# Six accumulation banks for the open chunks of the first propagation of batch 0, and a new place for its transposed means

## The reference

```
h  = relu(layernorm(x))
Xw = h @ Wv + bv;  sj = Xw @ aw[:d];  si = Xw @ aw[d:]
T  = adj * exp(leaky_relu(sj[j] + si[i] + ab));  T = T / (rowsum(T) + 1e-12)
H  = h @ Wk0 + bk0 + (T h) @ Wk1 + bk1 + (T T h) @ Wk2 + bk2
x1 = x + relu(H)
h  = relu(layernorm(x1));  A = adj + I;  dh = rsqrt(rowsum(A))
out = x1 + relu((dh A dh) h @ kernel + bias)
```

## Time and profile before

| | us |
|---|---|
| median of 3 runs (763.99 to 766.89) | 764.09 |
| the profiled execution | 765.5 |
| its span | 763.7 |
| TensorE busy | 749.1 (98%) |
| VectorE busy | 623.8 (82%) |
| ScalarE busy | 536.9 (70%) |
| GpSimd busy | 187.1 (24%) |

### The profile page before, as it was taken

How to read it: one execution, slowest core, us unless ns; L and a number is a source line. 1 busy time by engine, 2 the same in 40 slices (tenths; PEclk the granted TensorE clock), 3 DMA queues, 4 the chain that set the end, 5 groups by cost and what they waited for, 6 DMA issues and landing times.

```text
span 763.7 us, 14034 instructions
## 1 busy us (share of the span) xinstructions
PE 749.1 (98%) x5099; PEld 689.8 (90%) x5099; DVE 623.8 (82%) x1417; ACT 536.9 (70%) x1044; POOL 187.1 (24%) x190
## 2 busy tenths in 40 slices
PE   8879999999999999999999999999999999999997
PEld 8778998999889898998979999899998999889986
DVE  7877888978888789887998879897888877986665
ACT  3887796667966689557885678856696677956451
POOL 3023141222403224041321304122140222402330
PEclk9989999999999999999999999999999999999999
DMA  6557348753486445872657625776248654455511
GB/s 223 211 183 251 115 163 277 224 203 129 156 284 210 174 153 172 284 248 85 194 186 266 231 77 189 241 258 223 95 155 275 214 208 139 156 184 183 168 64 55
DMA packets 63909, 143.32 MB, mean 188 GB/s; under 512 B 6768, under 2 KB 32864, under 8 KB 63840
## 3 DMA queue, kind: packets, MB, share of 16 engines
q1 hardware_dynamic: 55072, 111.75, 43.9%
q10 hardware_dynamic: 8768, 30.68, 11.4%
HBM read 133.96 MB, written 8.45 MB: 186 GB/s over the span
## 4 chain that ended last, share of the span: by engine, by line
PE 94%; DVE 3%; ACT 1%; issue 1%; DMA 0%; POOL 0%; POOLq 0%; DVEq 0%; ACTq 0%
PE acc L1176 15%; PE acc L1178 15%; PE acc L1177 15%; PE da L1044 14%; PE db L1044 8%; PE da L1142 4%; PE tp L1142 4%; PE da L1144 4%; PE da L1143 4%; PE tp L1144 4%; PE tp L1143 4%; PE acc L1076 1%; PE acc L1195 1%; DVE t_raw L806 1%; PE acc L1197 1%
## 5 line engine op out<-in xcount | busy, mean ns | idle before, releaser
L1176 PE MATMUL acc<-g_hi,t_hi 128*128 128x256 f32 (+1 forms) x976 | 276.6, 283 | 0.1
L1178 PE MATMUL acc<-g_hi,t_lo 128*128 128x256 f32 (+1 forms) x976 | 275.2, 282 | 0.0
L1177 PE MATMUL acc<-g_lo,t_hi 128*128 128x256 f32 x976 | 274.6, 281 | 0.0
L1177 PEld LDWEIGHTS acc<-g_lo,t_hi 128*128 128x128 f32 x976 | 184.3, 189 | 0.4
L1176 PEld LDWEIGHTS acc<-g_hi,t_hi 128*128 128x128 f32 x976 | 183.8, 188 | 0.9 <-DVE g_lo L780 0.3
L1178 PEld LDWEIGHTS acc<-g_hi,t_lo 128*128 128x128 f32 x976 | 184.1, 189 | 0.0
L398 POOL TENSOR_TENSOR g_lo<-tmp,g_hi 128x256 fp32r<-128x256 f32 x64 | 61.9, 967 | 266.4 <-ACT g_hi L578 266.4
L817 DVE TENSOR_TENSOR a_lo<-a_raw,a_hi 128x512 fp32r<-128x512 f32 x128 | 94.1, 750 | 23.9 <-ACT a_hi L566 23.8
L523 ACT ACTIVATE tg_e<-si,sij 128x256 f32<-128x256 f32 x256 | 109.5, 501 | 0.1
L566 ACT CAST a_hi<-a_raw 128x512 fp32r<-128x512 f32 x128 | 76.8, 618 | 26.0 <-DVE a_raw L856 17.9
L404 POOL TENSOR_TENSOR hs_lo<-tmp,hs_hi 128x256 fp32r<-128x256 f32 x64 | 60.0, 957 | 89.7 <-ACT hs_hi L463 89.7
(11 more groups left out here) (153 smaller groups left out, 1615.4 us busy)
## 6 DMA issues: line engine op xcount, KB each, us to landing
a_raw<-adj_dram SPq DMA_DIRECT2D x64, 512.0 KB, 4.4
a_raw<-adj_z_dram SPq DMA_DIRECT2D x64, 512.0 KB, 4.3
tg_a<-adj_t_dram ACTq DMA_DIRECT2D x58, 512.0 KB, 4.3
x_o<-x_dram SPq DMA_DIRECT2D x64, 128.0 KB, 3.5
out_dram<-x_o SPq DMA_DIRECT2D x64, 128.0 KB, 4.0
x_nat<-x_dram SPq DMA_DIRECT2D x28, 256.0 KB, 4.9
xt<-x_t_dram SPq DMA_DIRECT2D x28, 256.0 KB, 5.4
si<-mean_rows_dram SPq DMA_DIRECT2D x7, 512.0 KB, 4.6
```

Source lines behind the costliest of these rows:

```text
L1176: nc.tensor.matmul(acc[:, s, 0:n], l_hi, r_hi, start=(jt == 0), stop=False)
L1177: nc.tensor.matmul(acc[:, s, 0:D], l_hi, r_lo, start=False, stop=False)
L1178: ins = nc.tensor.matmul(acc[:, s, 0:n], l_lo, r_hi, start=False, stop=(jt == NT - 1))
```

## The change

Chunks of phase U in batch 0 go round six banks, the three of `acc` and then `db`, `da` 0 and `da` 1, by a function `first_acc`; VectorE reads them there. In `accumulate_halves`, which only batch 0 uses, a chunk now waits for the read of the chunk six before it. The dense products of batch 1, which write `da` and `db`, begin only after six chunks of batch 0 have been read. The transpose of the means is issued between the second halves of chunks 2 and 3, not ahead of chunk 2's; ScalarE's copy of them is after `leaky(0, 6)`, not ahead of it. Other batches keep their banks.

```diff
+        FB = AB + OB
+
+        def first_acc(i):
+
+            return [acc[:, s] for s in range(AB)][i % FB] if i % FB < AB else out_bank[i % FB - AB]
...
             for u in range(HJ, NU - 1):
+                leaky(0, u)
                 if u == NU - 2:
                     mean_copy(1)
-                leaky(0, u)
                 exponent(0, u)
                 t_high(0, u - 1, False)
...
             def u_chunk(b, i):
-                s, a = i % 2, acc_slot(U_PHASE, i)
+                s = i % 2
+                ps = first_acc(i) if b == 0 else acc[:, acc_slot(U_PHASE, i)]
...
                 if b > 1:
 
                     pe.wait_ge(z_tmp_done, (b - 1) * NT)
+                else:
+
+                    pe.wait_ge(g1_tmp_ready, FB)
                 for g in range(NG):
...
-            def accumulate_halves(b, cp, middle):
+            def accumulate_halves(cp, middle):
 
                 for jh in range(2):
-                    pe.wait_ge(t_ready, b * NU + 2 * cp + jh + 1)
-                    if jh == 1 and middle is not None:
-                        middle()
+                    pe.wait_ge(t_ready, 2 * cp + jh + 1)
                     for i in (2 * cp, 2 * cp + 1):
-                        s = acc_slot(U_PHASE, i)
-                        if jh == 0 and i >= AB:
-                            pe.wait_ge(g1_tmp_ready, b * NT + i - AB + 1)
-                        elif jh == 0 and b > 0:
-                            pe.wait_ge(v_tmp_done, b * NT + i - AB + 1)
+                        if jh == 1 and i % 2 and middle is not None:
+                            middle()
+                        s = first_acc(i)
+                        if jh == 0 and i >= FB:
+                            pe.wait_ge(g1_tmp_ready, i - FB + 1)
```

More of the change, by code:

```diff
@@ L820, in u_chunk @@
             def u_chunk(b, i):
-                s, a = i % 2, acc_slot(U_PHASE, i)
+                s = i % 2
+                ps = first_acc(i) if b == 0 else acc[:, acc_slot(U_PHASE, i)]
                 dve.wait_ge(acc_full, b * PHASES + i + 1)
-                nc.vector.tensor_scalar_add(row_t[:, i:i + 1], acc[:, a, D:D + 1], EPS_ROW).then_inc(row_t_done, 1)
+                nc.vector.tensor_scalar_add(row_t[:, i:i + 1], ps[:, D:D + 1], EPS_ROW).then_inc(row_t_done, 1)
                 dve.wait_ge(row_t_done, b * NT + i + 1)
@@ L830, in u_chunk @@
                     dve.wait_ge(g1_ready, b * NT + i - 1)
-                nc.vector.scalar_tensor_tensor(out=tmp[:, s, :], in0=acc[:, a, 0:D], scalar=rinv[:, i:i + 1],
+                nc.vector.scalar_tensor_tensor(out=tmp[:, s, :], in0=ps[:, 0:D], scalar=rinv[:, i:i + 1],
                                                in1=p1[:, i, :], op0=ALU.mult, op1=ALU.add).then_inc(g1_tmp_ready, 1)
@@ L1179, in accumulate @@
                 ins.then_inc(acc_full, 1)
-            def accumulate_halves(b, cp, middle):
+            def accumulate_halves(cp, middle):
                 for jh in range(2):
-                    pe.wait_ge(t_ready, b * NU + 2 * cp + jh + 1)
-                    if jh == 1 and middle is not None:
-                        middle()
+                    pe.wait_ge(t_ready, 2 * cp + jh + 1)
                     for i in (2 * cp, 2 * cp + 1):
-                        s = acc_slot(U_PHASE, i)
-                        if jh == 0 and i >= AB:
-                            pe.wait_ge(g1_tmp_ready, b * NT + i - AB + 1)
-                        elif jh == 0 and b > 0:
-                            pe.wait_ge(v_tmp_done, b * NT + i - AB + 1)
+                        if jh == 1 and i % 2 and middle is not None:
[3 more added lines that the diff above has]
+                            pe.wait_ge(g1_tmp_ready, i - FB + 1)
                         for jt in range(jh * HJ, (jh + 1) * HJ):
                             l_hi, l_lo = t_hi[:, i, jt, :], t_lo[:, i, jt, :]
-                            nc.tensor.matmul(acc[:, s, 0:D + 2], l_hi, g2_hi[:, jt, :], start=(jt == 0), stop=False)
-                            nc.tensor.matmul(acc[:, s, 0:D], l_hi, g2_lo[:, jt, :], start=False, stop=False)
-                            ins = nc.tensor.matmul(acc[:, s, 0:D + 2], l_lo, g2_hi[:, jt, :], start=False, stop=(jt == NT - 1))
+                            nc.tensor.matmul(s[:, 0:D + 2], l_hi, g2_hi[:, jt, :], start=(jt == 0), stop=False)
+                            nc.tensor.matmul(s[:, 0:D], l_hi, g2_lo[:, jt, :], start=False, stop=False)
+                            ins = nc.tensor.matmul(s[:, 0:D + 2], l_lo, g2_hi[:, jt, :], start=False, stop=(jt == NT - 1))
                         if jh == 1:
@@ L1208, in batch @@
                         if i % 2 == 0:
-                            accumulate_halves(b, i // 2, (lambda: rows_of_mean(b + 1)) if b == 0 and i == 2 else None)
+                            accumulate_halves(i // 2, (lambda: rows_of_mean(1)) if i == 2 else None)
                         continue
```

## The result

The median went from 764.04 us (762.69 to 766.89, 6 runs) to 759.71 us (759.06 to 759.82, 6 runs): ratio 0.9942, 95% interval 0.9925 to 0.9959, so 4.3 us or 0.58% faster. The profiled execution took 759.82 us with a span of 758.0 (before: 765.5 and 763.7), 5.7 us less.

A forecast was written before the change was run, and what follows sets the result against it. TensorE alone bounds everything behind 67.7 us. 7.79 us of old waits and echoes go, less 1.2 of new waits and 0.54 at the dense stage; 6.1 us taken, forecast 758.0 us, range 756.6 to 760.9.

The forecast's parts named there:

- (c): Rival, chance 0.05: units of t stay late because their loads time them; only the second wait and echo go, 761 us.
- (d): Rival, chance 0.03, slower: the clock stays at 1.2 GHz from 48.1 on, dense stage 1.3 us later than before, 765.4 us.
- The two bank waits and their echoes go: TensorE, batch 0's first propagation: waits of 2.73 and 2.23 us for tmp and slow-clock echoes of 1.26 and 1.57 vanish, 7.79 us.
- Pair (2, 3), and the pause at 48: TensorE runs chunks 2 and 3 without waiting for the means, then idles 0.9 us at 48.1 for unit 4's low part.
- That a pause of 1 us leaves the clock: TensorE's new idle of 0.9 us at 48.1 is too short to drop the granted clock from 1.00.
- rival (a): Rival, chance 0.20: one of TensorE's new pauses drops the clock for some 3 us, time 758.8 to 759.6 us.
- ScalarE's queue: ScalarE loses its 3.53 us idle: unit 6's leaky pieces start at 44.94, mean copy follows, unit 6's high part from 51.77.
- VectorE's steps of 1.14 us and GpSimd's of 1.66: VectorE's products and low parts take 1.14 us, GpSimd's splits 1.66; TensorE's next waits for t are 0.1 and 0.2 us.
- The start of the dense stage: Batch 1's dense stage starts at 61.45 in place of 67.66, 6.2 us earlier, after a wait of 1.25 us for ht_lo.
- The new wait for six reads: Ahead of batch 1's dense stage: met at 58.2, while TensorE arrives at 60.2, so it costs nothing.
- Row tile 4 late, rival (b): Rival, chance 0.10: row tile 4's load lands late, ScalarE's second ht_hi up to 1.5 us late, time 759.5 us.
- From profile to median: Profiled time forecast at 759.4 us; the median before lay 1.4 us under its profiled execution, which gives 758.0.

The follow-up runs named there:

- E2: The two moves of the means alone (transpose and ScalarE's copy), on the kernel before with its three banks: 763.97 us, ratio 0.9994 to the kernel before.
- E1: The change with its six banks alone, the transpose and ScalarE's copy of the means put back in their old places: 759.62 us.
- E3: The whole change with four banks (acc and db) in place of six, the wait for all eight reads ahead of the first product into db: 759.55 us.
- E4: The whole change, with GpSimd's splits of chunks 0 and 1 placed in VectorE's reads of chunks 1 and 2: 758.91 us.
- E5: The whole change, with batch 1's first ht pair ahead of less urgent work on ScalarE and VectorE, row sums 3 and 4 one chunk later: 760.99 us.
- E7: E6 with batch 1's transposed x loaded behind unit 7's adjacency tile in place of after unit 4's: 761.71 us.
- E9: The whole change, with ScalarE's first ht_hi of batch 1 just ahead of row sum 3 and VectorE's first ht_lo ahead of its second centring: 760.26 us.
- E8: The whole change, with TensorE also waiting for chunk 1's read ahead of pair (4, 5), a pause of 1.83 us: 759.68 us.
- E11: The whole change, with TensorE waiting ahead of pair (4, 5) for VectorE's product of unit 6, a pause of 2.94 us in the profile: 761.47 us.
- E6: The whole change with the edits of E4 and E5 together: 759.52 us.
- E10: E4 and E9 together, plus, in batch 1, VectorE's third centring behind its first read of db and ScalarE's third ht_hi behind its second tile: 758.51 us.

## Why the prediction was right

Forecast 758.0 (756.6 to 760.9), measured 759.71: right in sign, mechanism and range; the saving, 6.1 forecast, was 4.3 by the medians and 5.7 by the two profiles. Rivals (c) and (d) did not happen: unit 5's low part was over at 51.91, and the clock stayed at 1.00. By its steps:

- *The two bank waits and their echoes go.* Right. E2 shows that without a further bank both stay, E1 that the moves of the means add nothing, and E3 that one further bank does it.
- *Pair (2, 3), and the pause at 48.* Right: transpose at 45.32, pause 1.33 against 0.9 forecast. 0.27 of the difference is the load of unit 5, for which product 5 waited until 45.95 in place of 45.68.
- *That a pause of 1 us leaves the clock.* Right in all runs of the change. What rival (a), at 0.20, wanted came only with pauses about twice as long: at 2.6 us three of ten executions had a lower mean clock, at 2.9 seven of nine.
- *ScalarE's queue.* Right to 0.3 us: leaky pieces 44.91 (44.94), copy 46.52 (46.69), unit 6's high part 51.57 (51.77). Of the means' moves I said that the old place of the transpose would cost TensorE 0.4; it costs 0.52 there and nothing in the end (E1).
- *VectorE's steps of 1.14 us and GpSimd's of 1.66.* This step failed. I took 1.66 from the earlier trace rows as what a split takes, and 1.14 as what a product or low part takes beside it. The split takes 0.75, and the rest of the 1.66 was waiting for VectorE. After the change two operations of VectorE with two inputs from SBUF stood one behind the other, the split got in between, and the second of them waited, 0.54 and 0.55 us. The waits at 52 and 55.6 became 0.47 and 0.45 in place of 0.1 and 0.2. E4 takes the cause away and gets 0.59 us back (1.03 of the stretch, less 0.44 for an earlier load). The 1.77 us stood in the trace of the kernel before, from batch 1 on.
- *The start of the dense stage.* 62.45 in place of 61.45: 0.27 from the load of unit 5; of the other 0.73 the lock explains 0.59 by E4. The wait for `ht_lo` was 0.85, not 1.25, since TensorE was later itself. ScalarE's row sums ahead of `ht_hi` were indeed late next together with VectorE's chain (E5 cuts this wait to 0.20).
- *The new wait for six reads.* Never seen; met at 59.0, TensorE was there at 61.6.
- *Row tile 4 late, rival (b).* Did not happen in the change. But behind the start of the dense stage there is little slack: E5, E7 and E9 had new waits there.
- *From profile to median.* I subtracted 1.4 us, by which the profile of before lay above its median, from both. After the change that distance is 0.1. It was not an offset that both kernels have, but one execution's place in the spread of the kernel before, 4.2 us wide over its six runs, and the change takes most of that spread away (0.8). This is the larger part of the miss: 1.3 of 1.7 us, and 0.4 between the forecast of the profiled time (759.4) and its measurement (759.82). The 0.4 was partly luck: the dense stage started 1.0 us later than forecast, and what lies behind it was 0.49 us shorter in the profile after than in that of before, which I had put at nothing. The low clock is a part of the spread: all 44 runs of the kernel before beside the experiments have it, from 0.998 down to 0.994, and the 17 at 0.996 or less took 765.5 us on average, the 27 above 763.6. The profiled execution of before, 765.5 at 0.996, was of the first kind. How large that part is the runs don't settle, since those at 0.998 alone reach from 763.06 to 764.88.

Behind the start of the dense stage the profile after took 695.55 us and that of before 696.04; E1 to E4, E8 and E11, which have no new waits there, took 695.76 to 696.05, so I don't read the 0.49 us as an effect of the change.

## What to carry to other kernels

Where one buffer is missing, count from when each chunk's predecessor is read: one bank more did here what three did, and the stall on a second engine was only its shadow. An operation's duration beside another engine can be mostly waiting; take its shortest instance as its work, look for longer ones in all batches, and ask who waits once something else stands behind it. Before a shorter stretch is put down to an edit, take out what varies by itself (here a load, 0.44 us of E4's 1.03). When the engine that bounds gets its data earlier, look for the next stage's first consumers before taking the time as won: of five versions that shortened the stretch further (E4, E5, E6, E9, E10), E5 came out slower than the change and E9 no faster (0.55 us slower by the medians, on a chip where the kernel before was 0.4 slower), E6 equal to it, and E10, with most reordering, kept about half of its last step.

## What the runs showed of the hardware that I had not expected

That a GpSimd operation and a VectorE operation with two inputs from SBUF hold each other up in whole instructions I had not expected when I forecast (E4). Whether a pause brings TensorE's low clock is a matter of the single execution: at 2.9 us seven of nine showed it, and the profiled one did not. At 1.3 and 1.8 us none of ten did. The mean granted clock of every run tells this where one profile misleads. And the spread of the kernel before goes partly with such echoes: with the long pauses gone, that of six runs fell from 4.2 to 0.8 us, though E8, at a clock of 1.0, still spread over 2.1.
